# Bias products of a routed tile on four row groups of TensorE instead of two

## The reference, cut to what matters

```python
lora_out = einsum('bsr,bdr->bsd', t, Bm); z = lora_out + lang_embed[language_ids][:, None, :]
h   = einsum('nd,edh->enh', xf, We1) + be1[:, None, :]      # xf = z as rows; HR = 768, so h has 1536
act = a * gelu(g)                                           # a, g = the two halves of h
yE  = einsum('enh,ehd->end', act, We2) + be2[:, None, :]
yr  = einsum('end,ne->nd', yE, w)                           # w: two weights per token
```

## Time and profile before

| | |
|---|---|
| median of 3 runs | 803.03 us (802.36 to 803.09) |
| profiled execution | 802.67 us, of which 800.9 us are the span of the profile |
| granted TensorE clock, mean | 0.995 |
| PE busy | 780.7 us, 97% of the span |
| DVE, ACT, POOL busy | 577.5, 298.9, 405.3 us |
| routed tiles | PE from 431 us to the end, 75 tiles |

### The profile page before, as it was taken

One profiled execution on the slowest core, in us unless ns is written; L12 is line 12 of the kernel. 1 busy time (PEld: TensorE's weight loads), 2 busy tenths in 40 slices (PEclk: granted clock), 3 DMA queues, 4 the chain that ended last, 5 costly groups with the idle time before them and its releaser, 6 DMA issues.

```text
span 800.9 us, 27814 instructions
## 1 busy us (share of the span) xinstructions
PE 780.7 (97%) x9379; PEld 658.8 (82%) x9380; DVE 577.5 (72%) x1382; ACT 298.9 (37%) x915; POOL 405.3 (51%) x511
## 2 busy tenths in 40 slices
PE   7999999999999999999999999999999999999994
PEld 6788888888888888777778888888888888888883
DVE  3999888888888788679885666666666666776661
ACT  1454444444444445542223333333333333333330
POOL 3143244444444444302011777777777777777762
PEclk9999999999999999999999999999999999999998
DMA  8553355555556564058733222332222322232222
GB/s 270 166 183 100 114 171 181 182 183 183 182 182 180 176 184 140 2 168 259 228 108 131 36 35 35 34 39 36 34 34 34 40 35 34 34 40 36 34 31 26
DMA packets 49325, 86.11 MB, mean 108 GB/s; under 512 B 7298, under 2 KB 27970, under 8 KB 49122
## 3 DMA queue, kind: packets, MB, share of 16 engines
q1 hardware_dynamic: 33778, 68.83, 27.1%
q0 software_dynamic: 13888, 15.13, 14.4%
q10 hardware_dynamic: 1584, 1.10, 0.5%
HBM read 68.48 MB, written 16.55 MB: 106 GB/s over the span
## 4 chain that ended last, share of the span: by engine, by line
PE 90%; DVE 5%; issue 2%; DMA 1%; SPq 1%; POOL 0%; DVEq 0%; ACT 0%
PE ps L1576 24%; PE ps L1563 13%; PE ps L1235 7%; PE ps L1474 6%; PE ps L1333 4%; PE ps L1557 4%; PE ps L1251 4%; PE ps L1307 3%; PE ps L1463 3%; PE ps L1280 3%; PE ps L1220 3%; PE ps L1544 2%; PE ps L1340 2%; PE ps L1293 2%; PE ps L1322 2%
## 5 line engine op out<-in xcount | busy, mean ns | idle before, releaser
L1576 PE MATMUL ps<-arena,stage 128*128 x900 | 206.6, 380 | 0.0
L1576 PEld LDWEIGHTS ps<-arena,stage 128*128 128x128 f32 x900 | 165.4, 190 | 19.4
L504 POOL DMA_INDIRECT out_dram<-stage,to_row x75 | 120.6, 1608 | 76.0 <-DVE stage L1144 67.2
L707 ACT ACTIVATE stage<-ps 128x384 f32<-128x384 f32 x150 | 65.4, 488 | 241.8 <-PE ps L1563 241.8
L1563 PE MATMUL ps<-token_rows,token_rows_T 64*128 64x128 f32 x1800 | 129.2, 272 | 0.0
L1563 PEld LDWEIGHTS ps<-token_rows,token_rows_T 64*128 64x128 f32 x1800 | 118.8, 189 | 1.7
L496 POOL DMA_INDIRECT token_rows<-gated_rows,from_row x75 | 75.0, 1001 | 61.2 <-DVE to_row L1023 38.5
L1118 DVE COPY token_rows<-ps 128x128 f32<-128x128 f32 x75 | 21.9, 292 | 110.7 <-PE ps L1545 110.7
L408 POOL TENSOR_TENSOR arena<-arena 128x256 f32<-128x256 f32 x32 | 23.4, 731 | 138.1 <-DVE arena L833 130.8
L1128 DVE TENSOR_TENSOR stage<-ps,stage 128x384 f32<-128x384 f32 x150 | 76.0, 549 | 1.8 <-ACT stage L707 1.8
L794 DVE TENSOR_REDUCE arena<-ps 128x8 f32<-128x512 f32 x64 | 43.9, 686 | 39.0 <-PE ps L1271 38.6
(11 more groups left out here) (173 smaller groups left out, 1470.7 us busy)
## 6 DMA issues: line engine op xcount, KB each, us to landing
stage<-in_we_dram SPq DMA_DIRECT2D x36, 512.0 KB, 4.8
arena<-in_cond_w_dram SPq DMA_DIRECT2D x64, 256.0 KB, 2.9
arena<-in_we_dram SPq DMA_DIRECT2D x12, 768.0 KB, 5.7
arena<-in_x_both_dram SPq DMA_DIRECT2D x31, 256.0 KB, 2.7
arena<-in_L_cond_bias_dram SPq DMA_DIRECT2D x64, 64.0 KB, 2.9
out_dram<-arena SPq DMA_DIRECT2D x32, 128.0 KB, 2.0
be_bc<-in_be_rows_dram SPq DMA_DIRECT2D x13, 192.0 KB, 3.8
gated_rows<-token_rows POOLq DMA_DIRECT2D x2, 1152.0 KB, 11.5
```

The source lines that it names most:

```text
L504: pool.indirect_dma_start(out_rows, bass.IndirectOffsetOnAxis(to_row[:, t:t + 1], 0), y_sb[t % YR], None, compute_op=ALU.add).then_inc(d_a ...
L707: nc.scalar.activation(g_sb[hf].rearrange("p (j n) -> p j n", n=P), first_out[1][:, :, hf, :], ACT.Gelu).then_inc(g_ok, 1)
L1576: last = mm(ps[:, 4 + s % 2, 0:D], actT_sb[s % 2][:, hf, j * P:(j + 1) * P], arena[:, ds(e * E2 + (NJ * hf + j) * D, D)], start=(hf == 0 a ...
```

## The change

In `first_layer`, the six bias matmuls of a tile (64 rows by 256 moving columns, bf16, two ahead of the main ones of each `j`) become twelve of 32 rows by 128 moving columns, one for each `j`, `g` and `hf`, all of them ahead of the first main matmul. The four of one `j` use the four row groups of the array. The main matmuls are the same 12, in the same order. In PSUM `hf` now chooses the bank: group `g`, half `hf` lies in bank 2g + hf, in its first 384 columns. Of the accumulation flags only `j` = 0 of the bias products has `start`, and only the last `j` of the main ones has `stop`.

In `rowT_copy`, the two masked copies of 128 x 128 become one plain copy of 128 x 128 to bf16, placed ahead of the f32 copy of the rank block, and `s_langT` has half its size.

```diff
-        s_langT = [cut(P).bitcast(bf16) for _ in range(2)]
+        s_langT = [cut(P // 2).bitcast(bf16) for _ in range(2)]
...
-        first_out = [ps[:, 2 * g:2 * g + 2, :].rearrange("p b n -> p (b n)")[:, 0:2 * HH].rearrange(
-            "p (j h n) -> p j h n", h=2, n=P) for g in range(2)]
+        first_out = [ps[:, 2 * g:2 * g + 2, 0:HH].rearrange("p h (j n) -> p j h n", n=P) for g in range(2)]
...
-                V.tensor_copy(s_rowT[s % 2], ps[:, 7, 0:P])
-                for hf in range(2):
-                    last = V.tensor_scalar(s_langT[s % 2][:, hf * P:(hf + 1) * P], ps[:, 7, P:2 * P],
-                                           col["half"][:, hf:hf + 1], None, ALU.mult)
-                last.then_inc(rowT_sb, 1)
+                V.tensor_copy(s_langT[s % 2], ps[:, 7, P:2 * P])
+                V.tensor_copy(s_rowT[s % 2], ps[:, 7, 0:P]).then_inc(rowT_sb, 1)
...
                 for j in range(NJ):
-                    at = slice(j * P, (j + 1) * P)
                     for g in range(2):
-                        mm(first_out[g][:, j].rearrange("p h n -> p (h n)"),
-                           w1bx[s % 2].bitcast(bf16)[64 * g:64 * g + 64, at],
-                           s_langT[s % 2][64 * g:64 * g + 64, :], start=True, stop=False)
+                        for hf in range(2):
+                            r = slice(64 * g + 32 * hf, 64 * g + 32 * hf + 32)
+                            mm(first_out[g][:, j, hf, :], w1bx[s % 2].bitcast(bf16)[r, j * P:(j + 1) * P],
+                               s_langT[s % 2][r, :], start=(j == 0), stop=False)
+                for j in range(NJ):
                     pe.wait_ge(w1x_ok[j], t + 1)
                     for hf in range(2):
                         for g in range(2):
                             last = mm(first_out[g][:, j, hf, :],
                                       w1x[s % 2][64 * g:64 * g + 64, j * CW + hf * P:j * CW + (hf + 1) * P],
-                                      s_rowT[s % 2][64 * g:64 * g + 64, :], start=False, stop=(hf == 1))
+                                      s_rowT[s % 2][64 * g:64 * g + 64, :], start=False, stop=(j == NJ - 1))
                 last.then_inc(h_ps, 1)
```

## The result

The changed kernel takes 804.87 us in the median (803.68 to 807.59, 20 runs), the kernel before 803.34 us over as many runs. The ratio is 1.0023, 95% interval 1.0016 to 1.0029: slower by 1.3 to 2.3 us. So the change makes the kernel slower by some 2 us. The forecast was 806.7 us, 3.4 above this median of the kernel before, with a range from 801.6 to 810.5.

A forecast was written before the change was run, and what follows sets the result against it. PE was taken to bound the kernel, busy 97% of the span. Per tile 0.12 + 0.17 + 0.195 = 0.485 us against 0.43, +3.7 us over 75 tiles, gave 806.7 us; range 801.6 to 810.5.

The forecast's parts named there:

- the change of shape into them: From 128 rows into the 32-row bias products: 0.12 us a tile, slightly dearer with four loads than the 0.11 before.
- three rounds: The twelve bias products as three rounds of four running at once: 0.17 us a tile, bounds 0.16 and 0.19, against 0.32.
- The 0.056 us of a round: Bias products: a round can follow the last after 0.056 us, from 36 bf16 loads of 128 columns in 2.01 us.
- The new change of shape, 32 to 64 rows: From bias into main products: a third drain a tile, 0.195 us, bounds 0.15 and 0.21, leading into f32 loads.
- The one row: L1208 (64 rows) before L1209 (5 rows): start 0.21 us later, load not ahead, taken as a change between row groups.
- DVE: Masked copies replaced by one plain copy: 22 us less busy in all, hidden by 0.75 us of slack, value nothing.
- The sum: First layer, changes of shape plus bias: 0.43 us before, 0.485 after, so +0.05 a tile and +3.7 over 75 tiles.
- the forecast's own 804.7 to 811: Whole kernel's time with the new drain at its full price; chance 0.64, with 806.7 us as its time.
- the second rival: Into main products: drain there, but its dear part mostly hidden (0.15 us); no change or slightly less, 802 to 803; chance 0.2.
- No drain between 32 and 64 rows: Bias into main products: passes freely, 0.29 us a tile instead of 0.434, -10.9 us, 792 us; chance 0.13.
- loads that serve one another in turn: Bias loads in four row groups queue: 0.67 us instead of 0.17 a tile, +41 us, 844 us; chance 0.02.
- a gain by DVE: PE waiting at first_layer: DVE's relief gains at most 0.3 us a tile less the 0.05, 784 us; chance 0.01.

The follow-up runs named there:

- e7_one_j: Changed kernel with only the j = 0 bias products, those of j = 1 and 2 left out; 0.9917 of the kernel before.
- e4_interleaved: Changed kernel with each j's four 32-row bias products put back directly ahead of that j's main ones; 1.0592 of the kernel before.
- e8_no_bias: Changed kernel with no bias products at all in the routed tiles; 796.0 us, 0.9916 of the kernel before.
- e6_mixed: Changed kernel with bias of j = 2 as four masked 64-row products directly ahead of the main ones, DVE's masked copies kept; 1.0036 of the kernel before.
- e12_bias_last: Changed kernel with its twelve 32-row bias products behind the main ones instead of ahead; 825.9 us, 1.0283 of the kernel before.
- e2_masks_kept: Changed kernel with DVE's two masked copies kept and read by the bias products; 805.74 us, 1.0034 of the kernel before.

## Why the prediction was right

**Bias products.** Forecast 0.12 us for the change of shape into them and 0.17 for three rounds. Measured 0.28, of which three rounds are 0.167 (`e7_one_j`), so 0.11 for the change: four loads cost no more than two. The term was 0.01 us a tile too dear, 0.7 us in all. The 0.056 us of a round were read off loads of the 128-row shape, not off one row group as the prediction says; that they hold for a round of four was an analogy, and it came true. A round of four is 14 ns a matmul. The Trainium skill (TensorE: Matmul & The Clock Gate, Part 1) gives about 25 ns as the least distance between two starts, and that does not hold between row groups here.

**The new change of shape, 32 to 64 rows.** Forecast 0.195 us; measured 1.54 - 1.35 = 0.19 to 0.20, in the changed kernel, in `e4_interleaved` three times a tile, and from 128 rows in `e8_no_bias`. It has two parts: the lag of 0.1 us, which every change has, and up to 0.1 us of f32 load that nothing covers. By the longest main record, this second part depends on what streams ahead in the same shape: 273 ns with 0.107 us of cover in the kernel before, 326 with 0.053 in `e6_mixed`, 373 with none here. The one row from which it was argued that row groups count as different shapes pointed the right way; by itself it was thin, and `e4_interleaved` is what shows it. The rule on drains in the Trainium skill (TensorEngine Tiling (Array Packing), Key Properties) holds here in both directions: 0.28 and 1.54 us whichever comes first (`e12_bias_last`).

**DVE.** Forecast nothing, and `e2_masks_kept` shows nothing. Its busy time fell by 13 us, not 22: the two lines of `rowT_copy` are 24 us less busy together, but a copy of weights behind them takes 4 us longer, and the rest is time in which DVE's records used to overlap.

**The sum.** Forecast +0.05 us a tile, +3.7 in all. Measured +0.042, and 3.14 over the stage. The time moved by less, 1.3 to 2.3 us, about half of the forecast, and 804.87 us is at the very edge of the forecast's own 804.7 to 811. The step that did not see this is the one from the tiles to the time: the prediction adds 3.7 us to the profiled execution and has no term for what comes behind PE's last matmul. That stretch ends with serial indirect adds, and 0.8 to 1.4 us of it in the kernel before go with where an instruction fetch falls, not with what was changed in the products. So the mechanism is borne out by the trace, to 0.01 us a tile; by the time alone it could hardly be told from the second rival, and that the time still fell on the forecast's side of it is partly luck.

**Rivals.** No drain between 32 and 64 rows, loads that serve one another in turn, and a gain by DVE are all excluded: the longest main matmul is 373 ns, twelve loads take 0.17 us, the masks are hidden. The half-hidden drain (second rival) is not this kernel, whose longest main record shows the full price, but it is what `e6_mixed` has.

## What to carry to other kernels

Splitting a matmul over more row groups pays by its streaming time, but if the work before and after is in another shape of the array, count one more change: here 0.1 us of lag, plus whatever of the next stretch's first load the stream ahead doesn't cover. Twelve matmuls that saved 0.15 us paid 0.195 for it. Each round saved 0.05 us, so three left a loss of 0.04 us a tile and, as an estimate from these figures, four would just break even and five would gain. The other way, to bring the neighbours into the same shape, was not tried.

Before shaving the engine that bounds a loop, look how far below it the next bound lies: here a serial chain of indirect adds sits at 4.64 us under a tile of 4.74, so of the 18 us that leaving out the bias should have given, 7 came.

Where a difference of a few tenths of a per cent is to be explained, measure a distance inside the trace that repeats (to 0.01 us here) beside the total, which scatters by 1 us.

## What the runs showed of the hardware

- An instruction fetch on the queue `q8` that begins 1.9 to 2.6 us after the issue of an indirect add goes with a landing after 4.3 to 5.2 us instead of 3.6 to 4.0, eight times in eight; one that begins up to 1.8 us after it, or from 3.1 us on, does not. On the other instruction queue, `q14`, the time of the start doesn't sort them so clearly. Twenty-four instructions more at 10 us of the kernel before moved the fetch from the next-to-last add, 0.8 to 1.4 us late, to the one ahead of it, 0.4 us late, and the time to 0.9988 (0.9979 to 0.9996). Forty-eight moved it clear of the transfer; that kernel is at 0.9994 (0.9984 to 1.0005). That only PE's program was changed suggests that the fetch is PE's. By what way it goes with a late add on another queue was not tried.
- Two of the 74 distances between indirect adds are long in every one of these traces of the kernel before and the changed one: the 37th (5.4 to 5.6 us) and the 72nd (5.1 to 5.4). The adds ahead of these distances land no later than others, and the cause is open.
- Twelve short bf16 matmuls behind 24 f32 records and ahead of the transposes let the second layer, two instructions later, start 0.2 us late and take about 0.1 us longer (`e12_bias_last`), while the same twelve ahead of the 24 don't. It is so inside the loop only; in tiles written out ahead of it the same order costs nothing.
